# A graph kernel's cosine pass: GpSimd prunes 512 of 3327 columns of each block, ScalarE sums them, and VectorE makes a row's threshold behind its pruning

## The chip, the cores and the metric

The kernel runs on one core of a Trainium2 chip. The metric is the device time of one launch in microseconds (us). Where several runs are given, it is their median.

## What is computed

Four graph layers work on 3327 nodes with 64 features each and a full adjacency matrix. The change lies in the fourth, which runs the function below twice (`it` is 0, then 1). Here `H` is the adjacency (3327 x 3327, float32):

```python
cos = xn @ xn.T                                     # xn: normalised rows of x_comp
edge_scores = softmax(cos * H / TAU, axis=1)
edge_mask = (edge_scores >= th_edge) & comp_mask[:, None]
H_pruned = H * edge_mask
connectivity = H_pruned.sum(axis=1)                 # sum of each row
node_scores = softmax(connectivity * feat_mag / TAU)
...
vdeg = maximum(H_pruned.sum(axis=1), EPS)
edeg = maximum(H_pruned.sum(axis=0), EPS)           # sum of each column
transformed = x_final @ W
agg = H_pruned.T * dv_isqrt[None, :] @ transformed  # the "down" pass
msg = dv_isqrt[:, None] * (H_pruned @ agg)          # the "up" pass
```

## The kernel before

The nodes are padded to 26 blocks of 128 rows (`NB` = 26). A block of the adjacency is 128 x 3328 float32, 1664 KB, and lies in a slot of SBUF while it is used. The adjacency doesn't fit, so that each pass (edge, att, cos, down, up, in this order, twice) streams it again from HBM. SyncE issues all loads from one queue, in the order of the passes; each waits until the slot's last user is done. The cosine pass has four slots (`slot0` to `slot3`), and its last four blocks stay in them for the down pass.

The cosine pass goes over the blocks k = 0 to 25. For each:

- TensorE makes the cosines in four pieces of 2 x 416 columns, in three buffers of PSUM. `piece_place` says which buffer, and how many pieces ago it was last used. In its queue the column sums of block k-2 (`columns`, which multiplies the pruned slot by ones) stand between the pieces: ahead of them are block k+1's first two pieces. When they are done, the slot is free for the load of block k+2 (`block_done`).
- VectorE multiplies each piece by the slot's columns into `prod[k % 2]` and takes its maximum (`product_piece`, L1311, shown as a CUSTOM instruction and an accumulator read). `product_max` (L1322) makes the row's maximum.
- ScalarE takes the exponentials in place with their row sum (L1063, `exps`).
- VectorE makes the threshold of a row in `cut` (L1449, `cut_of`): the row sum times `th_edge`, or something huge where the node is masked out.
- VectorE prunes the slot (L1457, `prune`): each element times (product >= threshold), and the row sum into `conn`. ScalarE takes the signs of product minus threshold into `arena` for the later passes (L1081), and says with `product_free` that the product buffer is free.

The work of two blocks overlaps: VectorE prunes block k-1 while ScalarE does block k's exponentials. The order on each engine is the order of the code, `cosine_pass` on VectorE. A first piece also waits for the pruning two blocks before, which reads the same product buffer.

Behind the pass, `conn` gives the node scores through a softmax, whose maximum and sum over the partitions GpSimd takes (L531, L533); before the change this is nearly all that GpSimd does. The down pass needs the features made from it. In these passes all engines' semaphore waits are written out by hand.

## Time and profile before

| | |
|---|---|
| time, median of 3 runs | 1784.53 us (1782.18 to 1786.14) |
| time of the profiled execution | 1784.21 us |
| its span, first to last instruction | 1782.4 us |
| TensorE busy | 1544.1 us (87%) |
| VectorE busy | 1195.5 us (67%) |
| ScalarE busy | 682.5 us (38%) |
| GpSimd busy | 4.0 us |
| the two cosine passes in the span | about 693 to 904 us and 1346 to 1555 us |
| mean granted TensorE clock | 0.95 of full speed |

An engine's share is over the whole span; the passes differ in what limits them, so the windows of a pass say more about it. The windows of the section below go from block 2's maximum to block 25's. In the profile, PE is TensorE, DVE is VectorE, ACT is ScalarE, POOL is GpSimd, SP is SyncE. What stands in brackets at the end of a timeline's row is the idle time of the engine before it and what ended it.

### The profile page before, as it was taken

The page shows a single profiled execution, that of the slowest core. Times are in us where ns is not written, and L with a number is a line of the kernel's source. Part 1 is how long each engine was busy: PE and PEld are TensorE (multiplying, and loading weights), DVE is VectorE, ACT ScalarE, POOL GpSimd, SP SyncE. Part 2 cuts the span into 40 slices and gives each one's busy share as a digit, 9 for nine tenths or more (in the row PEclk, how much of TensorE's full clock was granted, in tenths as well). Part 3 has the DMA queues.
Part 4 walks back from the last instruction along what each step waited for, and adds up shares of the span by engine and source line. Part 5 has one row for each costly group of instructions (what it writes and reads, how often), then busy time and mean ns, then how long its engine had stood idle before and what let it go on. Part 6 is the DMA issues. An engine that isn't in the chain of part 4 may idle for free.

```text
span 1782.4 us, 22339 instructions
## 1 busy us (share of the span) xinstructions
PE 1544.1 (87%) x9517; PEld 614.4 (34%) x9517; DVE 1195.5 (67%) x1684; ACT 682.5 (38%) x520; POOL 4.0 (0%) x17
## 2 busy tenths in 40 slices
PE   6789998999999998777787799999997777787895
PEld 2234433334443333222232344443333222232442
DVE  0000306777423997999988798027988999989897
ACT  0000101333113775777720242115666787700441
POOL 0000000000000000000000000000000000000000
PEclk9999999999999999878889999999999888799998
DMA  9979596799798993556569999999992566589994
GB/s 404 426 283 427 232 427 231 243 346 411 304 427 358 382 377 147 208 214 229 193 268 426 423 420 426 425 427 398 383 373 93 202 220 228 187 362 425 426 426 169
DMA packets 60611, 578.29 MB, mean 324 GB/s; under 512 B 6240, under 2 KB 6496, under 8 KB 20832
## 3 DMA queue, kind: packets, MB, share of 16 engines
q1 hardware_dynamic: 60512, 576.87, 80.9%
q8 instruction: 75, 1.23, 0.3%
q14 instruction: 24, 0.20, 0.0%
HBM read 575.14 MB, written 1.70 MB: 324 GB/s over the span
## 4 chain that ended last, share of the span: by engine, by line
PE 50%; DVE 28%; DMA 18%; ACT 2%; issue 2%; SPq 0%; DVEq 0%; POOL 0%; ACTq 0%
PE ps L548 47%; DVE pairs L1311 11%; DVE slot L1457 9%; DMA slot<-adj 9%; DMA arena<-adj_t 7%; DMA slot<-adj_t 2%; PE ps L891 2%; DVE slot L1485 1%; DVE slot L1499 1%; ACT pairs L1063 1%; DVE hats L1499 0%; DVE negmax L1322 0%; PE ps L590 0%; ACT arena L1081 0%; ACT hats L1100 0%
## 5 line engine op out<-in xcount | busy, mean ns | idle before, releaser
L1311 DVE CUSTOM_DVE_ANT_1 pairs<-ps,slot 128x832 f32<-128x832 f32 x352 | 345.5, 1021 | 29.8 <-PE ps L548 15.7
L548 PE MATMUL ps<-slot,cur 128*64 128x512 f32 (+1 forms) x1536 | 281.4, 515 | 31.6 <-DVE slot L1485 20.2
L548 PE MATMUL ps<-hats 64*128 64x416 f32 x832 | 224.7, 649 | 95.1 <-DVE max L1311 93.8
L1063 ACT ACTIVATE pairs<-pairs,negmax 128x3327 f32<-128x3327 f32 x88 | 270.3, 3071 | 71.5 <-DVE negmax L1322 71.3
L548 PE MATMUL ps<-arena 64*128 64x416 f32 (+1 forms) x1072 | 207.5, 524 | 0.4 <-DVE max L1311 0.4
L1081 ACT ACTIVATE arena<-pairs,cut 128x3328 fp8e4<-128x3328 f32 x52 | 159.9, 3074 | 87.2 <-DVE cut L1449 87.2
L1457 DVE SCALAR_TENSOR_TENSOR slot<-pairs,cut,slot 128x3327 f32<-128x3327 f32 x52 | 191.2, 3677 | 0.1
L548 PEld LDWEIGHTS ps<-slot,cur 128*64 128x64 f32 x1536 | 103.4, 137 | 205.6 <-issue 164.1
L548 PEld LDWEIGHTS ps<-hats 64*128 64x128 f32 x832 | 77.8, 215 | 233.0 <-DVE max L1311 184.7
L1131 DVE COPY pairs<-ps 128x512 f32<-128x512 f32 x3 | 2.1, 692 | 195.1 <-PE ps L548 195.1
L1100 ACT ACTIVATE hats<-ps 128x2048 int16<-128x2048 int16 (+1 forms) x28 | 42.1, 1556 | 231.3 <-PE ps L891 231.3
L548 PEld LDWEIGHTS ps<-arena 64*128 64x128 f32 (+1 forms) x1072 | 87.1, 175 | 121.3 <-DVE max L1311 62.4
L1485 DVE SCALAR_TENSOR_TENSOR slot<-arena,slot 128x3328 f32<-128x3328 int8 x28 | 101.5, 3626 | 19.2 <-DMA slot<-adj 19.2
L548 PE MATMUL ps<-slot,ones 128*32 128x416 f32 x832 | 106.3, 641 | 6.7 <-DVE slot L1457 6.7
L548 PE MATMUL ps<-pairs,hats 128*128 128x512 bf16 (+1 forms) x408 | 89.2, 341 | 7.1 <-DVE pairs L1264 4.3
L548 PE MATMUL ps<-pairs,arena 128*64 128x512 bf16 (+2 forms) x736 | 94.7, 372 | 0.1
L548 PE MATMUL ps<-slot,arena 128*64 128x512 f32 x480 | 88.4, 521 | 1.6 <-DMA slot<-adj 1.6
L1009 ACT ACTIVATE pairs<-ps 128x512 int16<-128x512 f32 x104 | 53.1, 517 | 92.5 <-PE ps L548 92.4
L1264 DVE TENSOR_SCALAR pairs<-ps 128x512 int16<-128x512 f32 x104 | 60.5, 590 | 36.3 <-PE ps L548 32.4
L942 ACT ACTIVATE pairs<-ps 128x640 f32<-128x640 f32 (+1 forms) x6 | 3.9, 652 | 198.4 <-PE ps L548 198.4
L1499 DVE SCALAR_TENSOR_TENSOR slot<-hats,slot 128x3328 f32<-128x3328 int8 x20 | 72.1, 3622 | 8.8 <-ACT hats L1100 5.8
L548 PE MATMUL ps<-arena,cur 128*64 128x512 f32 (+1 forms) x384 | 68.6, 513 | 1.1 <-DMA arena<-adj_t 1.0
(186 smaller groups left out, 1454.8 us busy)
## 6 DMA issues: line engine op xcount, KB each, us to landing
slot<-adj SPq DMA_DIRECT2D x162, 1664.0 KB, 8.9
slot<-adj_t SPq DMA_DIRECT2D x64, 1664.0 KB, 15.5
arena<-adj_t SPq DMA_DIRECT2D x26, 1664.0 KB, 23.5
arena<-adj_t SPq DMA_DIRECT2D x52, 832.0 KB, 6.5
arena<-adj SPq DMA_DIRECT2D x15, 1664.0 KB, 14.5
pairs<-adj SPq DMA_DIRECT2D x15, 1664.0 KB, 15.7
pairs<-adj_t SPq DMA_DIRECT2D x12, 1664.0 KB, 14.6
hats<-adj SPq DMA_DIRECT2D x8, 1664.0 KB, 15.0
```

The costliest lines, as they stand in the source:

```text
L548: return pe.matmul(o, l, r, start=start, stop=stop, skip_group_check=True)
L891: last = pe.transpose(ps[:, 4 * BANK + q * D:4 * BANK + (q + 1) * D].bitcast(BF16), sign_pairs[:, q * HALF + pair * P:q * HALF + (pair + 1 ...
L942: act.activation(agg_f[:, CHUNK_COLS[c]], ps[:, CHUNK_COLS[c]], ACT.Copy).then_inc(early_cols[c], 1)
L1009: act.activation(dst, bank(c, w), ACT.Relu).then_inc(relu_act, 1)
L1063: act.activation(bufs[b][:, 0:N], bufs[b][:, 0:N], ACT.Exp, bias=negmax[:, b:b + 1], accum_out=rowsum[:, b:b + 1]).then_inc(exp_done, 1)
L1081: act.activation(interleaved(sign_marks[:, row * NP:(row + 1) * NP]), halves(prod[k % 2][:, 0:NP]), ACT.Sign, bias=cut[:, k % 2:k % 2 + 1] ...
L1100: act.activation(turned[pair % 2][:, cols], ps[:, 4 * BANK:4 * BANK + HALF].bitcast(I16)[:, cols], ACT.Copy)\
L1264: dve.tensor_scalar(dst, bank(2 + c, w), 0.0, None, ALU.max).then_inc(relu_dve, 1)
L1311: dve.tensor_tensor_reduce(out=pieces3(bufs[k % len(bufs)], c), in0=pieces_psum(piece_place(name, k, c)[0]), in1=pieces3(slot_of(name, k), ...
L1457: dve.scalar_tensor_tensor(out=slot[:, 0:N], in0=prod[k % 2][:, 0:N], scalar=cut[:, k % 2:k % 2 + 1], in1=slot[:, 0:N], op0=ALU.is_ge, op1 ...
L1485: dve.scalar_tensor_tensor(out=slot, in0=interleaved(signs[:, row * NP:(row + 1) * NP]), scalar=0.0, in1=slot, op0=ALU.is_le, op1=ALU.mult ...
L1499: dve.scalar_tensor_tensor(out=slot, in0=interleaved(turned[k // 2 % 2].bitcast(I8))[:, k % 2], scalar=0.0, in1=slot, op0=ALU.is_le, op1=A ...
```

## The change

VectorE's pruning stops 512 columns before the end. GpSimd prunes these 512 in two instructions: marks (product >= threshold) into a tile of its own, then the slot's columns times the marks. ScalarE sums the 512 by row, one block late, behind the signs; the sums go into `conn_share`, which VectorE adds to `conn` behind the pass. In VectorE's queue a block's threshold moves from behind the next block's first piece to ahead of it, right behind the pruning. The waits that this needs are added: TensorE's column sums wait for GpSimd too, SyncE's loads for ScalarE's sum, and a piece for the marks two blocks before, which read its product buffer.

```diff
+SHARE = 512
...
@@ SyncE, late_stream
                     sp.wait_ge(block_done, EARLY_RING + free)
+                    behind = free - 1 - BASE[f"cos{it}"]
+                    if kind in ("cos", "down") and 0 <= behind < NB:
+                        sp.wait_ge(share_summed, it * NB + behind + 1)
...
@@ GpSimd
+            def prune_share(it, k):
+                slot = slot_of(f"cos{it}", k)
+                cols = slice(N - SHARE, N)
+                pool.wait_ge(row_cut, it * NB + k + 1)
+                if it * NB + k:
+                    pool.wait_ge(share_pruned, it * NB + k)
+                pool.tensor_scalar(share_marks[:, :], prod[k % 2][:, cols], cut[:, k % 2:k % 2 + 1], None, ALU.is_ge)\
+                    .then_inc(share_marked, 1)
+                pool.wait_ge(share_marked, it * NB + k + 1)
+                pool.tensor_tensor(slot[:, cols], slot[:, cols], share_marks[:, :], ALU.mult).then_inc(share_pruned, 1)
...
             for it in range(2):
                 node_softmax(2 * it)
+                for k in range(NB):
+                    prune_share(it, k)
                 node_softmax(2 * it + 1)
...
@@ TensorE, columns
                         pe.wait_ge(pruned, it * PRUNES + k + 1)
+                        pe.wait_ge(share_pruned, it * NB + k + 1)
...
@@ ScalarE
+                def sum_share(k):
+                    at = place(ROW_ORDER["cos"][k])
+                    act.wait_ge(share_pruned, it * NB + k + 1)
+                    if it * NB + k:
+                        act.wait_ge(share_summed, it * NB + k)
+                    act.activation(share_sink[:, :], slot_of(f"cos{it}", k)[:, N - SHARE:N], ACT.Copy,
+                                   accum_out=small["conn_share"][:, at:at + 1]).then_inc(share_summed, 1)
                 for k in range(NB):
                     exp_and_sign(k)
+                    if k:
+                        sum_share(k - 1)
+                sum_share(NB - 1)
...
@@ VectorE, product_piece
                             dve.wait_ge(pruned, g // 2 * PRUNES + k - 1)
+                            dve.wait_ge(share_marked, g // 2 * NB + k - 1)
...
@@ VectorE
             def cosine_pass(name, cut_of, prune):
                 for k in range(NB):
-                    product_piece(name, k, 0)
-                    if k > 1:
-                        cut_of(k - 1)
-                    for c in range(1, 4):
+                    for c in range(4):
                         product_piece(name, k, c)
                     if k == 1:
                         cut_of(0)
                     product_max(name, k)
                     if k:
                         prune(k - 1)
-                cut_of(NB - 1)
+                        cut_of(k)
                 prune(NB - 1)
...
-                    dve.scalar_tensor_tensor(out=slot[:, 0:N], in0=prod[k % 2][:, 0:N],
-                                             scalar=cut[:, k % 2:k % 2 + 1], in1=slot[:, 0:N], op0=ALU.is_ge,
+                    cols = slice(0, N - SHARE)
+                    dve.scalar_tensor_tensor(out=slot[:, cols], in0=prod[k % 2][:, cols],
+                                             scalar=cut[:, k % 2:k % 2 + 1], in1=slot[:, cols], op0=ALU.is_ge,
                                              op1=ALU.mult, accum_out=S["conn"][:, at:at + 1]).then_inc(pruned, 1)
...
                 dve.wait_ge(pruned, it * PRUNES + NB)
+                dve.wait_ge(share_summed, it * NB + NB)
+                link(dve.tensor_tensor(S["conn"], S["conn"], S["conn_share"], ALU.add))
```

On VectorE, from block 2's maximum to block 3's, the queue held this before (L1322 is the maximum, L1457 the pruning, L1311 a piece and its accumulator read, L1449 the threshold):

```order
L1322 TENSOR_REDUCE negmax<-max4 128x1 [waits piece_read]
L1457 SCALAR_TENSOR_TENSOR slot3,conn<-pairs,cut,slot3 128x3327 [waits row_cut]
L1311 ISA pairs,max4<-ps,slot1 128x2x416 [waits pruned,piece_ready,product_free,slot_loaded1]
L1311 ISA max4 128x1
L1449 SCALAR_TENSOR_TENSOR cut<-rowsum,blocked 128x1 [waits exp_done]
L1311 ISA pairs,max4<-ps,slot1 128x2x416 [waits piece_ready]
```

And it holds this now, at the same place (L1360, L1493, L1349 and L1484 are the same four):

```order
L1360 TENSOR_REDUCE negmax<-max4 128x1 [waits piece_read]
L1493 SCALAR_TENSOR_TENSOR slot3,conn<-pairs,cut,slot3 128x2815 [waits row_cut]
L1484 SCALAR_TENSOR_TENSOR cut<-rowsum,blocked 128x1 [waits exp_done]
L1349 ISA pairs,max4<-ps,slot1 128x2x416 [waits share_marked,pruned,piece_ready,product_free,slot_loaded1]
L1349 ISA max4 128x1
L1349 ISA pairs,max4<-ps,slot1 128x2x416 [waits piece_ready]
```

The threshold, with its wait for the exponentials, moved ahead of the next block's first piece, and that piece waits for one semaphore more.

On ScalarE, at the end of a pass, the queue held this before (L1063 exponentials, L1081 signs, L1070 the softmax's exponentials):

```order
L1063 ACTIVATE pairs,rowsum<-pairs,negmax 128x3327 [waits negmax_ready]
L1081 ACTIVATE arena<-pairs,cut 128x2x1664 [waits row_cut]
L1063 ACTIVATE pairs,rowsum<-pairs,negmax 128x3327 [waits negmax_ready]
L1081 ACTIVATE arena<-pairs,cut 128x2x1664 [waits row_cut]
L1070 ACTIVATE node_e,psum_<-node_z,ngmax 128x26 [waits soft_bias]
```

It holds this now (L1089, L1107, L1096 are these three, L1116 the new row sums):

```order
L1089 ACTIVATE pairs,rowsum<-pairs,negmax 128x3327 [waits negmax_ready]
L1107 ACTIVATE arena<-pairs,cut 128x2x1664 [waits row_cut]
L1116 ACTIVATE share_sink,conn_share<-slot1 128x512 [waits share_summed,share_pruned]
L1089 ACTIVATE pairs,rowsum<-pairs,negmax 128x3327 [waits negmax_ready]
L1107 ACTIVATE arena<-pairs,cut 128x2x1664 [waits row_cut]
L1116 ACTIVATE share_sink,conn_share<-slot2 128x512 [waits share_summed,share_pruned]
L1116 ACTIVATE share_sink,conn_share<-slot3 128x512 [waits share_summed,share_pruned]
L1096 ACTIVATE node_e,psum_<-node_z,ngmax 128x26 [waits soft_bias]
```

One row sum follows each block's signs, and two follow the last.

On GpSimd, at the same place, there are now the last blocks' marks (L546) and products (L549) ahead of the softmax's two reductions (L554, L556). Before, its queue held the reductions alone:

```order
L546 TENSOR_SCALAR share_marks<-pairs,cut 128x512 [waits share_pruned,row_cut]
L549 TENSOR_TENSOR slot2<-slot2,share_marks 128x512 [waits share_marked]
L546 TENSOR_SCALAR share_marks<-pairs,cut 128x512 [waits share_pruned,row_cut]
L549 TENSOR_TENSOR slot3<-slot3,share_marks 128x512 [waits share_marked]
L554 ISA
L554 ISA gmax<-pmax 128x1 [waits part_max]
L556 ISA gsum<-psum_ 128x1 [waits part_sum]
```

The row "L554 ISA" without operands tells GpSimd to change the set of functions that it runs; another stands ahead of the first marks of each pass. Before the change there is one in the whole program, at its start.

## Rows read from the trace of the kernel before

**Rows 1.** The page: each engine's busy time; the chain that ended last, by line.
```profile
PE 1544.1 (87%) x9517; PEld 614.4 (34%) x9517; DVE 1195.5 (67%) x1684; ACT 682.5 (38%) x520; POOL 4.0 (0%) x17
...
PE ps L548 47%; DVE pairs L1311 11%; DVE slot L1457 9%; DMA slot<-adj 9%; DMA arena<-adj_t 7%; DMA slot<-adj_t 2%; PE ps L891 2%; DVE slot L1485 1%; DVE slot L1499 1%; ACT pairs L1063 1%; DVE hats L1499 0%; DVE negmax L1322 0%; PE ps L590 0%; ACT arena L1081 0%; ACT hats L1100 0%
```

**Rows 2.** Windows: length, busy PE PEld DVE ACT POOL, granted clock, DMA share, GB/s.
```profile
710.50:896.30 185.80, 141.78 (x740) 45.12 (x742) 177.17 (x277) 142.50 (x70) 0.00 (x0) 0.83 0.56 202
1363.50:1547.10 183.60, 144.10 (x744) 45.39 (x746) 177.02 (x278) 142.39 (x70) 0.00 (x0) 0.83 0.57 205
```

**Rows 3.** Timeline, VectorE, one block: start, length in us, instruction.
```profile
742.38 0.16 DVE L1322 TENSOR_REDUCE negmax<-max 128x1 f32<-128x4 f32 x1
...
746.38 1.02 DVE L1311 CUSTOM_DVE_ANT_1 pairs<-ps,slot 128x832 f32<-128x832 f32 x1 [0.24 <-DMA slot<-adj]
...
747.32 0.15 DVE L1449 SCALAR_TENSOR_TENSOR cut<-rowsum,blocked 128x1 f32<-128x1 f32 x1
747.40 1.02 DVE L1311 CUSTOM_DVE_ANT_1 pairs<-ps,slot 128x832 f32<-128x832 f32 x1
...
750.35 0.16 DVE L1322 TENSOR_REDUCE negmax<-max 128x1 f32<-128x4 f32 x1
```

**Rows 4.** Timeline, ScalarE, the same block.
```profile
742.57 3.07 ACT L1063 ACTIVATE pairs<-pairs,negmax 128x3327 f32<-128x3327 f32 x1
745.55 0.19 ACT L1063 ACTIVATION_READ_ACCUMULATOR pairs<-pairs,negmax 128x1 f32 x1
747.51 3.07 ACT L1081 ACTIVATE arena<-pairs,cut 128x3328 fp8e4<-128x3328 f32 x1 [1.78 <-DVE cut L1449]
```

**Rows 5.** Groups by line and form: count, busy us, mean ns, idle before.
```profile
L1457 DVE SCALAR_TENSOR_TENSOR slot<-pairs,cut,slot 128x3327 f32<-128x3327 f32 x52 | 191.2, 3677 | 0.1
L1449 DVE SCALAR_TENSOR_TENSOR cut<-rowsum,blocked 128x1 f32<-128x1 f32 x52 | 8.0, 155 | 2.4 <-ACT pairs L1063 2.4
L1063 ACT ACTIVATION_READ_ACCUMULATOR pairs<-pairs,negmax 128x1 f32 x88 | 16.5, 188 | 0.0
L958 ACT ACTIVATE arena<-arena 128x512 f32<-128x512 f32 x8 | 5.0, 629 | 16.2 <-DVE arena L1141 16.2
L1063 ACT ACT_TABLE_LOAD x2 | 2.6, 1283 | 0.0
```

**Rows 6.** Timeline, start of the first pass.
```profile
707.27 0.19 ACT L1063 ACTIVATION_READ_ACCUMULATOR pairs<-pairs,negmax 128x1 f32 x1
...
707.50 0.16 DVE L1449 SCALAR_TENSOR_TENSOR cut<-rowsum,blocked 128x1 f32<-128x1 f32 x1 [1.20 <-ACT pairs L1063]
```

**Rows 7.** Groups of GpSimd.
```profile
L531 POOL PARTITION_ALL_REDUCE gmax<-pmax x4 | 1.4, 351 | 1549.4 <-DVE pmax L1368 1549.4
L523 POOL MEMSET ones_b<- 128x512 bf16 x1 | 0.5, 530 | 0.0
```

**Rows 8.** Timeline, end of the first pass.
```profile
896.26 0.16 DVE L1322 TENSOR_REDUCE negmax<-max 128x1 f32<-128x4 f32 x1
...
903.85 0.19 DVE L1465 TENSOR_TENSOR imp<-conn,norm 128x26 f32<-128x26 f32 x1
```

**Rows 9.** Timeline, TensorE: column sums (slot,ones), pieces (hats); a window, columns as above.
```profile
736.56 2.86 PE L548 MATMUL ps<-slot,ones 128*32 128x416 f32 x16
...
742.36 1.60 PE L548 MATMUL ps<-slot,ones 128*32 128x416 f32 x16
...
747.46 0.97 PE L548 MATMUL ps<-hats 64*128 64x416 f32 x4 [2.60 <-DVE max L1311]
...
734.00:736.00 2.00, 2.00 (x8) 0.63 (x4) 1.97 (x4) 2.00 (x2) 0.00 (x0) 0.50 0.02 7
```

**Rows 10.** Issues of loads (timeline), and one in the chain (us to landing).
```profile
739.49 0.33 SPq L483 DMA_DIRECT2D slot<-adj  x1
...
852.01 8.40 DMA slot<-adj
...
1535.37 0.33 SPq L483 DMA_DIRECT2D slot<-adj  x1
```

More of the change, by code:

```diff
@@ L242, in build_program @@
                  ("mean", "var", "structural", "colsum", "imp", "comp", "blocked", "norm", "rnorm",
-                  "conn", "node_z", "node_e", "dv", "edeg")}
+                  "conn", "conn_share", "node_z", "node_e", "dv", "edeg")}
         tiny = {n: sb(n, 1, F32) for n in ("pmax", "gmax", "ngmax", "psum_", "gsum", "thr", "query_shift")}
         max4 = sb("max4", 2 * 4, F32)
+        share_marks = sb("share_marks", SHARE, BF16)
+        share_sink = sb("share_sink", SHARE, BF16)
         row_rz = sb("row_rz", 3, F32)
@@ L376, in build_program @@
         pruned = sem("pruned")
+        share_marked = sem("share_marked")
+        share_pruned = sem("share_pruned")
+        share_summed = sem("share_summed")
         product_free = sem("product_free")
@@ L480, in late_stream @@
                         sp.wait_ge(pruned, it * PRUNES + NB)
+                        sp.wait_ge(share_pruned, it * NB + NB)
                         sp.wait_ge(product_free, (2 * it + 2) * NB + 2)
```

## The prediction

> **What bounds the kernel now.** I read the page first: TensorE is busy 87% of the span and VectorE 67%, and the chain that ended last goes to VectorE's pieces and to its pruning (L1457) with 11% and 9% [rows 1]. Such shares are averages over stages, so I then asked for the windows of the two cosine passes from their third block on. There VectorE works 177.17 of 185.80 us and 177.02 of 183.60 us, ScalarE 142 us and TensorE 142 to 144 us at a mean granted clock of 0.83, and the DMA engines are a little over half busy [rows 2]. So in this stage VectorE sets the pace. The timeline of one block shows how [rows 3, 4]. Count from the start of the block's maximum M (742.38): the pruning of the block before starts at once, the next first piece at M+4.00 (746.38), then comes the threshold (747.32, which moves the second piece back by 0.08), and the next maximum is at M+7.97 (750.35). Of 24 such periods in a pass nearly all are 7.96 to 7.98 long. ScalarE's exponentials start at M+0.19 and their sum is read at M+3.36 (745.55 plus 0.19); the reader should see that the threshold, and the signs behind it, wait for nothing but their place in VectorE's queue: the signs start at 747.51, after 1.78 us in which ScalarE idled [rows 4].
>
> **VectorE's block after the change.** The pruning takes 3677 ns for 3327 columns and an instruction of that kind on one column 155 ns [rows 5], so 1.059 ns a column: 512 columns fewer save 0.54 us. By the queue alone the next first piece then starts at M+3.46. The threshold now stands ahead of it and needs the exponentials' sum: M+3.36, plus 0.04 until VectorE has it (at the pass's start the sum is read at 707.46, the threshold starts at 707.50 [rows 6]), plus 0.07 to 0.08 until the piece behind it starts (747.32 to 747.40): M+3.47. The two ends meet, so this wait costs 0.01. From the first piece to the maximum it takes 3.97, without the threshold in it 3.89. The period is 3.47 + 3.89 = 7.36, say 7.37. Of the 23 periods from block 2's maximum to block 25's, which took 185.7 us and 183.6 us [rows 2], 169.5 us each would be left: 16.2 + 14.1 = 30.3 us saved, if nothing else is late.
>
> **ScalarE.** Signs start at M+3.58 (0.18 behind the threshold), and what is behind them 2.97 later (745.55 less 742.57 is the pitch of an instruction of this length): M+6.55. A 512-column pass from tile to tile takes 629 ns, the reading of a sum 188 ns [rows 5], together about 0.73 of pitch: it ends at M+7.28. The next exponentials want to start at M+7.56. It is hidden with 0.28 to spare; every tenth above that would cost 0.1 x 46.
>
> **GpSimd.** Nothing in this trace has GpSimd read a wide tile. The nearest rows are a memset of 512 columns, 530 ns, and a reduction of one column over partitions, 351 ns [rows 7]. From below, two instructions at 0.53 take 1.1; with the second at twice that for its two inputs, 1.6; with semaphores 1.8. From above there is no row: the pair is hidden while it is shorter than the next block's pieces (3.9 us), because until then only TensorE's column sums (which wait for the later VectorE pruning anyway), ScalarE's sum and a piece two blocks on wait for it. I take 1.8 because the memset is the nearest row, and cost it at nothing. SyncE's new waits are in order behind ones that end later: ScalarE's sum ends at M+7.3 of the following block, the column sums behind that.
>
> **The pass's ends.** At the start, exponentials of block 1 are held up by the signs of block 0, and the threshold waits 1.20 us until 707.50 [rows 6], but one piece has run ahead of it. Now this piece is behind the threshold: 0.94 more, in each pass. At the end, today the last maximum is at 896.26 and the first step of the softmax at 903.85: M+7.59 [rows 8]. Now the last threshold is at M+3.40, the signs end their pitch at M+6.55, and two row sums of 0.73 and 0.78 follow, one behind the other: M+8.06; then the new addition, 0.04 + 0.23: M+8.33. That is 0.8 more, in each pass, and all that follows (softmax, features, the down stage with its loads) waits for it. Both ends and both passes: 2 x (0.94 + 0.8) = 3.5 us lost.
>
> **What is late next: the loads.** A slot is loaded again when TensorE has summed its columns. In every other block that sum stands behind two pieces that wait for VectorE. When the granted clock is 0.50 (1.2 GHz) the sum takes 2.86 us instead of 1.60, and ends 5.0 us behind the maximum at 734.41 (742.38 less a period): the load goes out at 739.49 [rows 9, 10], and block 7's first piece at 746.38 had its landing as releaser [rows 3]: 6.8 us later, M+11.9. Before the change that was just in time (two periods less 3.97 is 11.97). After it, it is wanted at 7.37 + 3.47 = M+10.85. Of the 20 such loads (ten a pass, 739.49 first, 1535.37 last [rows 10]) I took landing less maximum: most lie at 10.6 to 11.9, two at 12.7 and 13.6 (852.01, 8.40 to landing, which stalls the kernel now). Beyond 10.87 they add up to 7.9 us in the first pass and 3.8 in the second: 11.7 us of the gain go if TensorE's slow stretches stay as they are. If none is left, such a load goes out at M+2.6 and nothing is lost. The clock falls after TensorE has idled 2.60 us, run one piece of 0.97 and idled again (747.46 [rows 9]), and VectorE's shorter pruning takes about 0.5 of those 4.6 us away: same shape, a little less idle. So I stay near the upper end and take 9.
>
> Sum: -30.3 + 3.5 + 9.0 = -17.8 us. The profiled execution took 1784.2 us, 0.3 under the median of the three, so 1766.4 by its own time and 1767 against the median.
>
> **Rivals.** First, the clock no longer falls in most blocks: the 9 go and 1757.7 is left. For it speaks that TensorE's idle stretches shorten, against it that each late load makes a new one. Chance 0.15.
>
> Second, the ends of the pass cost more, because GpSimd is not ready. GpSimd has to change its set of functions before the first product of a pass and again ahead of the softmax's maximum. The first change has over 10 us of cover, the second only from the last product (M+5.4) to the maximum (M+9.1), 3.7 us. The nearest row is ScalarE's loading of a table, 1283 ns [rows 5]: hidden if it begins with the change, 2.6 us in both passes if it begins with the call. In the last block, too, VectorE's pruning starts together with GpSimd's marks; if one of them has to wait for the other, 0.5 to 1.1 us are added and the row sum slips as much: 2 us for both passes. Together 1768 to 1771. But the table is another engine's; a GpSimd load five times as long, 6.4 us from each of two calls on, adds 12.8: 1780. Chance 0.2. The Trainium skill, "GPSIMD Engine Reference", section Instruction dispatch, puts the first call of a freshly loaded function at about 6 us more; beginning with the change that would be 2.2 us a pass, beginning with the call 6 us a pass; no row here shows it. The Trainium skill, "SBUF — State Buffer", section Who interferes with whom, says that a VectorE instruction with two SBUF inputs and a GpSimd instruction that reads SBUF exclude each other for their whole length. The pieces have one input in PSUM, so by that rule GpSimd's work is free where I have put it, and costs where a pruning runs beside it: at the last block, and everywhere if the pair is longer than 3.9 us.
>
> Third, no change: TensorE's slow stretches grow until every second load binds and two blocks take 15.9 us as now. Only the ends remain, +3.5 us, 1788, at the edge of what can be told. Chance 0.07: the rows of loads speak against it, as their path alone allows 15.8 and mostly less.
>
> Fourth, slower: GpSimd is far from the memset's pace. Its products then run into VectorE's next pruning, or set the pace themselves. The point is 7.97 us for the pair with its semaphores, 3.9 for one instruction, seven times the memset. At 9 us a pair, 46 periods of 9 instead of 7.97 are 47 us, 1835. Chance 0.08; another 0.03 for smaller losses of the same kind, between 3.9 us and the point. The forecast keeps 0.47.
>
> **Numbers.** 0.2% (3.6 us) is about what can be told from no change here. Faster: forecast, first and second rival, 0.82. Same: 0.07. Slower: 0.11. The range goes from the first rival to the end of the second, 1756 to 1780, and leaves out the third and fourth. For the forecast alone it would be 1760 to 1772.
>
> **What would show it.** VectorE's period from maximum to maximum 7.37 where no load is late; the pruning 3.13; the threshold's idle before it below 0.1; first pieces of every second block with the load as releaser, 0.3 to 1 us. ScalarE: row sums 0.63 long and no maximum that waits for it. GpSimd's pair near 1.8 us and done before the next maximum. From the last maximum to the softmax's first step 8.3. Wrong would be the forecast if GpSimd's instructions are several times as long, if VectorE's pieces stretch beside them, or if the clock changes.

## The result, and the profile after

The changed kernel took 1796.18 us (median of four, 1793.98 to 1801.87), the kernel before on the same chip 1784.79 us: ratio 1.0071, 95% interval [1.0051, 1.0091]. It is slower by 11 us, where the prediction had 1767 us, 18 less. The profiled execution took 1801.87 us, the longest of the changed kernel's four, so that the sums below, made between the two profiles, come to +17.7 us instead of +11.4. The other three have no trace, so that it isn't shown in which stages the 6.3 us between the two sums lie. One execution of e3 below took 3291.44 us, at a granted clock of 1.0 and for a reason that the record doesn't show, and its ratio leaves it out.

The page answers to [rows 1]: GpSimd now works 153.8 us, and ScalarE's exponentials (L1089) have gone from 1% of the chain to 5%, while VectorE's pruning (L1493) has left it.

```profile
PE 1539.0 (86%) x9489; PEld 616.0 (34%) x9517; DVE 1173.0 (65%) x1686; ACT 715.9 (40%) x624; POOL 153.8 (9%) x121
...
PE ps L573 50%; DMA slot<-adj 12%; DVE pairs L1349 8%; DMA arena<-adj_t 7%; ACT pairs L1089 5%; DMA slot<-adj_t 2%; PE ps L917 2%; DVE slot L1522 1%; DVE slot L1536 1%; DVE pairs L1301 1%; POOL share_marks L546 1%; PE ps L842 0%; PE ps L615 0%; DVE hats L1536 0%; ACT arena L1107 0%
```

The windows from block 2's maximum to block 25's, which answer to [rows 2]: 185.80 us became 179.29 and 183.60 became 178.98. That is 11.1 us gained, a little over half of the 21.3 that the prediction had left here (30.3 less 9.0 for the loads). The granted clock is nearly as it was (0.83 and 0.85, before 0.83 twice), and GpSimd's 61 us lie beside the others.

```profile
712.39:891.68 179.29, 141.12 (x746) 44.86 (x746) 167.19 (x277) 157.41 (x115) 60.96 (x46) 0.83 0.58 210
1374.07:1553.05 178.98, 139.88 (x750) 44.78 (x746) 167.13 (x276) 157.41 (x115) 61.00 (x46) 0.85 0.58 210
```

**One block.** On VectorE's timeline (answers to [rows 3]) the maximum comes every 7.53 us where no load is late, not every 7.37. The threshold starts at M+3.39 (761.51), after 0.16 us in which VectorE waited for ScalarE, and the piece at M+3.63, 0.24 behind the threshold.

```profile
758.12 0.16 DVE L1360 TENSOR_REDUCE negmax<-max 128x1 f32<-128x4 f32 x1
758.20 3.14 DVE L1493 SCALAR_TENSOR_TENSOR slot<-pairs,cut,slot 128x2815 f32<-128x2815 f32 x1
...
761.51 0.16 DVE L1484 SCALAR_TENSOR_TENSOR cut<-rowsum,blocked 128x1 f32<-128x1 f32 x1 [0.16 <-ACT pairs L1089]
761.75 1.02 DVE L1349 CUSTOM_DVE_ANT_1 pairs<-ps,slot 128x832 f32<-128x832 f32 x1
...
765.65 0.16 DVE L1360 TENSOR_REDUCE negmax<-max 128x1 f32<-128x4 f32 x1
```

The chain through the same block says who sets this pace: it goes maximum, exponentials with the reading of their sum (L1089, x2), threshold, then a semaphore instruction of VectorE's queue (DVEq) and the piece. The pruning is not on it.

```profile
758.12 0.17 DVE negmax L1360
...
758.31 3.17 ACT pairs L1089 x2
...
761.51 0.06 DVE cut L1484
761.57 0.05 issue
761.62 0.05 DVEq L1348
761.67 0.08 issue
761.75 1.02 DVE pairs L1349
```

VectorE's waits in the first of the two windows: the 0.16 us comes in each of the 23 blocks, and what is lost to late loads (and to TensorE's pieces behind them) is 4.9 + 1.2 us. In the second window it is 3.7 again, and 4.4 + 1.4 us.

```profile
DVE pairs L1349 <- DMA slot<-adj: 4.9, 4, 1.6
DVE cut L1484 <- ACT pairs L1089: 3.7, 23, 0.2
DVE pairs L1349 <- PE ps L573: 1.2, 4, 0.4
```

The groups (as in [rows 5]): pruning 3143 ns as forecast; marks and product (L549) 1562 (median of 52) and 1090 ns, together 2.65 us against the 1.8 taken, but still hidden. The pair took half as much again as estimated, and in the blocks that cost nothing. The mean of 1789 ns for the marks is raised by four of about 4.5 us, the first and the last block's of each pass (702.11, 895.33, 1363.80 and 1556.70).

```profile
L1493 DVE SCALAR_TENSOR_TENSOR slot<-pairs,cut,slot 128x2815 f32<-128x2815 f32 x52 | 163.4, 3143 | 0.1
L546 POOL TENSOR_SCALAR share_marks<-pairs,cut 128x512 bf16<-128x512 f32 x52 | 93.0, 1789 | 267.9 <-DVE cut L1484 267.9
```

**The end of the pass** holds most of the loss. Before the change, the reduction over the partitions and the matmuls behind the softmax stood like this, the last maximum being at 896.26:

```profile
904.57 0.35 POOL L531 PARTITION_ALL_REDUCE gmax<-pmax  x1 [215.38 <-DVE pmax L1368]
907.90 1.53 PE L816 MATMUL ps<-cst,pairs 128*128 128x128 f32 x12 [1.00 <-ACT pairs L1090]
```

The timeline of all engines in the changed kernel, first pass, answers to them and to [rows 8]:

```profile
891.68 0.16 DVE L1360 TENSOR_REDUCE negmax<-max 128x1 f32<-128x4 f32 x1
...
895.26 3.15 DVE L1493 SCALAR_TENSOR_TENSOR slot<-pairs,cut,slot 128x2815 f32<-128x2815 f32 x1
895.33 4.51 POOL L546 TENSOR_SCALAR share_marks<-pairs,cut 128x512 bf16<-128x512 f32 x1 [6.25 <-DVE cut L1484]
...
899.92 1.09 POOL L549 TENSOR_TENSOR slot<-slot,share_marks 128x512 f32<-128x512 f32 x1
...
902.09 0.19 DVE L1502 TENSOR_TENSOR imp<-conn,norm 128x26 f32<-128x26 f32 x1
...
902.54 0.18 DVE L1403 TENSOR_REDUCE pmax<-node_z 128x1 f32<-128x26 f32 x1
...
910.96 0.38 POOL L554 PARTITION_ALL_REDUCE gmax<-pmax  x1 [9.94 <-issue]
...
914.31 2.82 PE L842 MATMUL ps<-cst,pairs 128*128 128x128 f32 x12 [7.45 <-ACT pairs L1127]
```

Three things stand here. The last marks began 0.07 us behind a pruning and took 4.51 us. The reduction over the partitions had its input at 902.73 and began at 910.96, 8.2 us later, with nothing but "issue" as the cause (time in which the engine waited for nothing that the profile shows). And the matmuls of the next stage, behind 7.45 us of idle, took 2.82 us at a granted clock of 0.50 (914.31 to 917.13); before, twelve of them took 1.53 at 1.00 (907.90 to 909.40). In the second pass the input is there at 1564.10 and the reduction starts at 1570.99, 6.9 us later:

```profile
1570.99 0.38 POOL L554 PARTITION_ALL_REDUCE gmax<-pmax  x1 [8.60 <-issue]
```

From the last maximum to the reduction it was 8.31 and 8.30 us before, now it is 19.28 and 17.94. That is 20.6 us more, of which 15.1 are the reduction's wait behind its input and 5.5 are the later input.

The 9.94 and 8.60 us are the change of functions, as e1 to e3 below show: the list of L554's instructions has two waits of this kind, one a pass, and the instruction that orders a change, the last at 1562.6; the first pass's stands at 901.24 in the trace.

```profile
L554 POOLq MODIFY_POOL_CONFIG  x6: 11/11/11, 1.6 to 1562.6; - x6
...
  issue: 18.5, 2
```

From the order to the first call that is 9.7 and 8.4 us.

### The profile page after: what moved, and what is told of

Same layout as the page of the kernel before. It is cut to its first block, busy times and chain, and to the rows that moved or that the text cites. A ratio compares the mean times of both kernels' runs of the same rounds, so it can differ in the third digit from the quotient of the medians.

```text
span 1799.8 us, 22731 instructions
## 1 busy us (share of the span) xinstructions
PE 1539.0 (86%) x9489; PEld 616.0 (34%) x9517; DVE 1173.0 (65%) x1686; ACT 715.9 (40%) x624; POOL 153.8 (9%) x121
## 4 chain that ended last, share of the span: by engine, by line
PE 53%; DMA 21%; DVE 16%; ACT 6%; issue 2%; POOL 1%; SPq 0%; DVEq 0%; ACTq 0%
PE ps L573 50%; DMA slot<-adj 12%; DVE pairs L1349 8%; DMA arena<-adj_t 7%; ACT pairs L1089 5%; DMA slot<-adj_t 2%; PE ps L917 2%; DVE slot L1522 1%; DVE slot L1536 1%; DVE pairs L1301 1%; POOL share_marks L546 1%; PE ps L842 0%; PE ps L615 0%; DVE hats L1536 0%; ACT arena L1107 0%
## 5 line engine op out<-in xcount | busy, mean ns | idle before, releaser
L1349 DVE CUSTOM_DVE_ANT_1 pairs<-ps,slot 128x832 f32<-128x832 f32 x352 | 342.8, 1020 | 30.9 <-PE ps L573 18.3
L1089 ACT ACTIVATE pairs<-pairs,negmax 128x3327 f32<-128x3327 f32 x88 | 270.0, 3069 | 105.5 <-DVE negmax L1360 105.5
L573 PE MATMUL ps<-hats 64*128 64x416 f32 x832 | 220.2, 642 | 91.6 <-DVE max L1349 90.4
L1107 ACT ACTIVATE arena<-pairs,cut 128x3328 fp8e4<-128x3328 f32 x52 | 159.8, 3072 | 12.7 <-DVE cut L1484 12.7
L1493 DVE SCALAR_TENSOR_TENSOR slot<-pairs,cut,slot 128x2815 f32<-128x2815 f32 x52 | 163.4, 3143 | 0.1
L1522 DVE SCALAR_TENSOR_TENSOR slot<-arena,slot 128x3328 f32<-128x3328 int8 x28 | 101.5, 3625 | 23.8 <-DMA slot<-adj 23.8
L546 POOL TENSOR_SCALAR share_marks<-pairs,cut 128x512 bf16<-128x512 f32 x52 | 93.0, 1789 | 267.9 <-DVE cut L1484 267.9
L554 POOL PARTITION_ALL_REDUCE gmax<-pmax x4 | 1.5, 364 | 1143.0 <-DVE pmax L1403 1124.5
```

What stands on the lines that cost most here:

```text
L546: pool.tensor_scalar(share_marks[:, :], prod[k % 2][:, cols], cut[:, k % 2:k % 2 + 1], None, ALU.is_ge)\
L573: return pe.matmul(o, l, r, start=start, stop=stop, skip_group_check=True)
L1089: act.activation(bufs[b][:, 0:N], bufs[b][:, 0:N], ACT.Exp, bias=negmax[:, b:b + 1], accum_out=rowsum[:, b:b + 1]).then_inc(exp_done, 1)
L1107: act.activation(interleaved(sign_marks[:, row * NP:(row + 1) * NP]), halves(prod[k % 2][:, 0:NP]), ACT.Sign, bias=cut[:, k % 2:k % 2 + 1] ...
L1349: dve.tensor_tensor_reduce(out=pieces3(bufs[k % len(bufs)], c), in0=pieces_psum(piece_place(name, k, c)[0]), in1=pieces3(slot_of(name, k), ...
L1493: dve.scalar_tensor_tensor(out=slot[:, cols], in0=prod[k % 2][:, cols], scalar=cut[:, k % 2:k % 2 + 1], in1=slot[:, cols], op0=ALU.is_ge, ...
```

## The experiments

Each ratio is to runs of the kernel before on the same chip: 1784.53 us for e1 to e4, 1785.20 for e6, e7, e9 and e10, 1784.45 for e5, e8 and e11, 1785.37 for e12. In the diffs the counts of the semaphore waits, which follow from the number of shared blocks, are left out, and the constants for the first and the last shared block are written as numbers.

**e1: no share in the last two blocks.** VectorE prunes blocks 24 and 25 whole; GpSimd is finished, and its functions are changed back, about two blocks earlier.

```diff
-                for k in range(NB):
+                for k in range(24):
                     prune_share(it, k)
...
-                    cols = slice(0, N - SHARE)
+                    cols = slice(0, N - SHARE if k < 24 else N)
```

> The change, but blocks 24 and 25 of each pass are pruned whole by VectorE as before, so that GpSimd's last product of a pass is that of block 23. Theory (switch): what costs is GpSimd's change of its set of functions behind its last product: 9.7 us until the softmax's maximum can start, 8.2 of them exposed, and about 2.5 more in which TensorE works at a granted clock of 0.50 after that wait. Here the change begins some 13 us earlier and is hidden; the marks of the last block, stretched from 1.56 to 4.5 us beside VectorE's pruning, fall away too (3 us). Expected 2 x (8.2 + 2.5 + 3) less 2 x 1.1 for the whole prunings: 26 us under the changed kernel, about 1770, faster than before. Rival (port alone): only the stretched marks matter: 6 us less, 1790. Rival (body): the loss is in the pass itself: no gain, 1796.

1772.35 us (1768.62 to 1778.36), ratio 0.9927 [0.9912, 0.9942]. Two blocks a pass, four of 52, turn 0.7% slower into 0.7% faster: 23.8 us. GpSimd's rows at this pass's end say where: the reduction now waits for its input and for nothing else.

```profile
900.54 0.38 POOL L566 PARTITION_ALL_REDUCE gmax<-pmax  x1 [19.07 <-DVE pmax L1417]
```

From the last maximum (891.96) to it are 8.58 us, in the second pass 8.57. The change of functions is ordered at 1531.0 in the second pass, 17 us ahead of the reduction, and can't be seen. The bodies (the windows from block 2's maximum to block 25's) are as in the changed kernel: 179.53 and 179.22 us.

**e2: the kernel before, and one GpSimd instruction behind the last threshold.** It works on a single column, which nobody reads; its own semaphore is left out below.

```diff
             for it in range(2):
                 node_softmax(2 * it)
+                pool.wait_ge(row_cut, it * NB + 26)
+                pool.tensor_scalar(tick[:, :], eps_t[:, :], 2.0, None, ALU.mult)
                 node_softmax(2 * it + 1)
```

> The kernel before, with one GpSimd instruction more in each pass: a one-column tensor_scalar that waits for the last threshold. It computes nothing that is used. It makes GpSimd change its set of functions twice a pass, the second time ahead of the softmax's maximum, at about 4.1 us behind the last row maximum. Switch theory: the maximum over partitions then starts 9.7 us later, at 13.8 instead of 8.3, and the clock's fall adds about 2: 7 to 8 us a pass, 1800. Rival (the delay came from long instructions before it, not from the change): within 1 us of before, 1785.

1804.88 us, ratio 1.011 [1.0096, 1.0125]: 20 us for two instructions on one column each, against the 14 to 16 expected. From the last maximum to the reduction are 16.70 and 17.50 us. GpSimd's timeline:

```profile
899.67 3.72 POOL L542 TENSOR_SCALAR tick<-eps_t 128x1 f32<-128x1 f32 x1 [210.74 <-DVE cut L1455]
912.44 0.38 POOL L533 PARTITION_ALL_REDUCE gmax<-pmax  x1 [9.06 <-issue]
```

The change alone, with no pruning moved, costs nearly all that the end lost: 17.6 us up to the reduction, where the changed kernel lost 20.6. The row also shows the other price: this instruction ran beside a pruning (899.60 to 903.28) and ended 0.11 us behind it.

**e3: the same instruction behind the threshold of block 15.** The edit is e2's with 16 in place of 26.

> As e2_switch_late, but the extra instruction waits for the threshold of block 15, some 80 us ahead of the softmax. Switch theory: the same changes of the set of functions are made, but hidden: as before, 1785 within 2. Rival (a change costs wherever it stands, for instance because loading the functions disturbs other engines or loads): 5 us or more above before.

1784.79 us, ratio 0.9998 [0.999, 1.0007]. The instruction takes 0.27 us, the reduction comes 83.41 us behind it and starts with its input. A change of functions costs nothing when nobody calls for 83 us, and in e1 nothing could be seen of it with 17 us; how little is enough was not tried. It also says that the loading doesn't begin with the call, else it would be seen here too.

**e4: the changed kernel with the old order of the thresholds** (the first piece of block k+1 ahead of the threshold of block k).

```diff
-                    for c in range(4):
+                    product_piece(name, k, 0)
+                    if k > 1:
+                        cut_of(k - 1)
+                    for c in range(1, 4):
                         product_piece(name, k, c)
...
-                        cut_of(k)
+                cut_of(NB - 1)
```

> The changed kernel with the threshold back behind the next block's first piece, as before; the share of GpSimd and ScalarE stays. By VectorE's queue a period is 7.97 less 0.54 = 7.43 us, where the changed kernel has 7.53, and the piece at the pass's start runs ahead again (1 us a pass): 46 x 0.10 + 2 = 6 to 7 us less, 1790. Rival: ScalarE's signs and row sum slip behind with the threshold, its exponentials start 0.7 us late in each block and something waits for them: period 7.6 or more, 1798 or more.

1793.96 us (1788.52 to 1802.25), ratio 1.0056 [1.0035, 1.0077]: 2.2 us less than the changed kernel, where 6 to 7 were expected, and the intervals overlap. The period where no load is late is 7.42 us, the starts (from the first maximum to block 2's) take 13.29 instead of 14.47, but more blocks wait for loads: the bodies are 180.75 and 180.12 us, longer than with the new order. (This profile too, 1802.25 us, is the longest of its kernel's.) Beyond 46 periods of 7.42 us that is 19.5 us of late loads, where the changed kernel has 11.9 beyond 46 of 7.53. So the shorter period couldn't be cashed while the loads were late.

**e5: the kernel before with the new order alone** (the edit to `cosine_pass` of the change, nothing else).

> The kernel before with the new order alone: the threshold of block k is made behind the pruning of block k-1 instead of behind the first product piece of block k+1; VectorE still prunes all 3328 columns and GpSimd and ScalarE do nothing new. Theory of the waits: a product piece directly behind a threshold loses about 0.1 to 0.2 us a block, because its own waits are worked off behind the threshold (in the changed kernel the piece began 0.23 us behind the threshold, 7.53 us a block against 7.42 with the old order). Then a block takes 8.05 to 8.15 us instead of 7.97, the stretch from the first maximum to the third grows from 13.3 to about 14.4 us in each pass, some of the body's loss is taken back by the late loads, and the kernel takes 1790 to 1795 us. Rival: the 0.11 us belongs to the share's own waits (the one on share_marked ahead of the piece), not to the order; then a block takes 7.97 us and only the two starts are lost, 1787 us.

1787.62 us, ratio 1.0016 [1.0007, 1.0025]. Both forecasts of the period missed (the rival's time, 1787, came for another reason than it gave): it is 7.89 us in most blocks, so the order itself gives 0.07 to 0.08 back, as the prediction had it. VectorE's timeline:

```profile
759.38 0.16 DVE L1322 TENSOR_REDUCE negmax<-max 128x1 f32<-128x4 f32 x1
759.46 3.68 DVE L1454 SCALAR_TENSOR_TENSOR slot<-pairs,cut,slot 128x3327 f32<-128x3327 f32 x1
...
763.06 0.15 DVE L1446 SCALAR_TENSOR_TENSOR cut<-rowsum,blocked 128x1 f32<-128x1 f32 x1
763.38 1.02 DVE L1311 CUSTOM_DVE_ANT_1 pairs<-ps,slot 128x832 f32<-128x832 f32 x1 [0.17 <-issue]
```

Here the threshold stands directly behind the pruning, at M+3.68, and has no wait; the piece is at M+4.00, where it was before the change. With the threshold ahead of it or without, it starts 0.24 us behind the pruning's end (763.14; before 746.14 and 746.38), so the threshold runs in time that passes anyway. The kernel is slower all the same because of the starts (14.44 instead of 13.30 us, twice), which the bodies (184.70 and 182.55 us) just about return, and because of the 1.3 us that the two passes lose from the reduction to the down pass. Whether that belongs to the order is not shown: e10, whose ends are those of the kernel before, has 1.1 there.

**e6: e1, with the piece's waits on the marks, the product buffer and the load put ahead of the threshold.**

```diff
                     if k:
                         prune(k - 1)
+                        if k + 1 < NB:
+                            g = PRODUCTS.index(name)
+                            dve.wait_ge(product_free, g * NB + k + 2)
+                            dve.wait_ge(share_marked, ...)
+                            landed(dve, name, k + 1)
                         cut_of(k)
```

> e1_share24 with three of the waits of a first piece (product buffer, marks, landing) moved ahead of the threshold in VectorE's queue; they are then passed while VectorE prunes or the exponentials run. In the changed kernel the piece starts 0.23 us behind the threshold's start where I had taken 0.07. Theory: the sequencer works off the piece's waits one after the other, behind the threshold that has just been let go, at some 0.04 each: the period falls from 7.53 to about 7.41, 46 x 0.12 = 5 us less than e1_share24, at most, and less where loads bind: 1768 to 1772. Rival: the 0.23 is the wait for the draining of the pruning, which stays where it was: period 7.53, no gain.

1776.96 us (1772.07 to 1780.09), ratio 0.9955 [0.9943, 0.9967]; a miss, and the rival's period: 7.53 us. The threshold started at M+3.49 instead of M+3.39, and the piece where it had been. The median is 4.6 us above e1's at the same period; while loads come late the runs of one such kernel spread over 8 to 14 us. The profiles show how: e6's, the shortest of its six, has 5.6 us beyond 46 periods of 7.53, e1's, the longest of its six, 12.4. More than that I can't say of it.

**e11: e7 (below), with the piece's wait for the pruning ahead of the threshold.** The edit is one line, a wait on `pruned`, moved from `product_piece` to ahead of `cut_of(k)`.

> From e7, with the wait of the product piece on the pruning of the block before put ahead of the threshold instead of behind it. If the 0.23 us between threshold and piece is this wait being worked off, the piece comes nearer to the threshold and the threshold doesn't move: a period of about 7.44 us, 1760 us. Rival, by e6_waits_first, where a moved wait only delayed the threshold by what it saved behind it: 7.53 us, 1763 to 1764 us, and the 0.2 us is a price of having waits between two instructions, wherever they stand.

1768.05 us, ratio 0.9905 [0.9889, 0.992]; both numbers missed, it is slower than either. The chain of one block:

```profile
759.07 3.17 ACT pairs L1104 x2
...
762.27 0.02 DVEq L1498
762.29 0.04 issue
762.34 0.06 DVE cut L1501
...
762.57 1.02 DVE pairs L1365
```

With a second wait ahead of it, the threshold no longer waits for the exponentials itself: a semaphore instruction does, and the threshold follows 0.07 us behind that, at M+3.46. The piece kept its distance (0.23), and the period became 7.59 us. e6 and e11 together: in neither was a wait that was moved ahead of the instruction on the path hidden, although what it waited for had happened before (in e11 the pruning ended at 762.09, the exponentials at 762.25).

**e12: e7 with a share of 384 columns instead of 512.**

> e7 with GpSimd's share cut from 512 columns to 384, so that VectorE's pruning takes 0.14 us more. e5 (the order alone, 7.89 us a block) and the changed kernel (7.53) differ by 0.36 us, though the pruning is 0.54 us shorter; 0.16 to 0.18 us are missing. Theory: with the shorter pruning the threshold no longer stands behind VectorE's pruning but waits for ScalarE's row sum, until 3.39 us behind the maximum, and the first piece starts 0.23 us behind the threshold; the sum of ScalarE, not the pruning, sets the period. By e5's distances the pruning of 2944 columns would let the piece start 3.60 us behind the maximum, the threshold lets it start at 3.62: the period stays 7.52 to 7.54 us and the time that of e7, 1763 to 1765 us. Rival: VectorE's own queue sets the period, and the 0.16 us is the price of the additional wait on share_marked: then the period grows by the whole 0.14 us to 7.66, 46 x 0.14 = 6 us, 1769 to 1770 us.

1765.77 us (1764.87 to 1766.94), ratio 0.9893 [0.9876, 0.9909], against 1763.67 of e7. The theory's period came, 7.53 us in nearly all blocks of both passes, its time (1763 to 1765) not quite; the median is 2 us above e7's, where the rival wanted 6, and the ratios' intervals overlap. VectorE's timeline:

```profile
758.30 0.16 DVE L1377 TENSOR_REDUCE negmax<-max 128x1 f32<-128x4 f32 x1
758.38 3.27 DVE L1510 SCALAR_TENSOR_TENSOR slot<-pairs,cut,slot 128x2943 f32<-128x2943 f32 x1
...
761.69 0.16 DVE L1501 SCALAR_TENSOR_TENSOR cut<-rowsum,blocked 128x1 f32<-128x1 f32 x1
761.93 1.02 DVE L1366 CUSTOM_DVE_ANT_1 pairs<-ps,slot 128x832 f32<-128x832 f32 x1
...
765.84 0.16 DVE L1377 TENSOR_REDUCE negmax<-max 128x1 f32<-128x4 f32 x1
```

The pruning is 0.13 us longer, the threshold stays at M+3.39, the piece (761.93) at M+3.63. In this order ScalarE's sum sets the pace, and a quarter of GpSimd's work bought nothing.

**e7: e1, and six matmuls on zeros behind TensorE's pieces in every second block.** They add zero to a buffer of PSUM and fill part of the time in which TensorE idles.

```diff
                         if k + 1 < NB:
                             piece(k + 1, 2)
+                        if (k + 1) % 2 == 1:
+                            for _ in range(6):
+                                mm(bank(6), zeros_b[:, :], ones_b[:, :], start=False)
```

> e1_share24 with six TensorE products of zeros (512 columns, added to the column sums' banks, so that nothing changes) behind the third piece of every second block, in the gap in which TensorE idles. Theory (clock): TensorE's granted clock stays up in the passes, column sums take 1.6 instead of 2.9 us, loads go out 2 us earlier and no first piece waits for a landing: the 12.4 us of a body beyond 23 x 7.53 in two passes go, e1 less 10 or so: 1762. Rival (the loads are late by the DMA rate): the clock rises but the stalls stay: 1772. Second rival: the products of zeros delay pieces: slower than 1775.

1763.67 us (1761.78 to 1765.39), ratio 0.988 [0.9868, 0.9893]: 8 to 9 us less than e1. The windows from block 2's maximum to block 25's:

```profile
710.83:884.65 173.82, 143.04 (x822) 44.53 (x818) 166.82 (x276) 157.41 (x115) 58.34 (x44) 0.97 0.61 216
1351.31:1524.44 173.13, 142.26 (x822) 44.38 (x818) 166.72 (x277) 157.41 (x115) 58.33 (x44) 0.98 0.61 217
```

The granted clock is 0.97 and 0.98 instead of 0.83 and 0.85, and 23 x 7.53 = 173.2 us: the late loads are gone, and one wait of 0.6 us for a piece of TensorE's is all that VectorE still loses beside the threshold's. TensorE was never short of time; at 1.2 GHz its column sums gave the slots back too late. In the block whose maximum is at 734.97 in the changed kernel the sum took 2.74 us and the next load went out at M+4.96; in the same block of e7 (maximum at 734.11) it took 1.60 us and the load went out at M+2.59.

**e10: the same matmuls in the kernel before.**

> The kernel before with the same products of zeros. Clock theory: there, loads stall VectorE only 2.6 and 0.5 us beyond its period in the two passes, so at most 3 us are to be had: 1782 to 1785. If it gains more, the products of zeros help outside the cosine pass, and e7_fill has to be read against this.

1782.44 us, ratio 0.9987 [0.9978, 0.9995]. Before the change there was little to give back: the two bodies stood 3.2 us above 46 periods of 7.96, and now stand 0.8 above. The filler is worth 8 to 9 us only together with the shorter period.

**e9: e1, with the marks held back until the next block's maximum,** so that they run beside a pruning.

```diff
                 pool.wait_ge(row_cut, it * NB + k + 1)
+                pool.wait_ge(negmax_ready, (2 * it + 1) * NB + k + 2)
```

> e1_share24, but GpSimd's marks of block k also wait for the maximum of block k+1, so that they start together with VectorE's pruning of block k instead of ahead of it. Port theory: VectorE's pruning, which has two inputs in SBUF, keeps GpSimd's marks out for its whole length: marks of 4.5 to 4.7 us instead of 1.56 in all 48 cases. A first piece two blocks on waits for them: about M+4.8 instead of 3.6, so the period grows to 8.6 or more and the kernel to 1772 + 46 x 1.1 = 1820 or more. Rival (the stretched marks are only those next to a change of GpSimd's functions): marks 1.56, over at M+1.8, before the pruning is; period 7.53, 1772.

1822.42 us, ratio 1.0212 [1.0199, 1.0225]. GpSimd's groups by form:

```profile
L559 POOL TENSOR_SCALAR share_marks<-pairs,cut 128x512 bf16<-128x512 f32 x48 | 207.6, 4326 | 180.5 <-DVE negmax L1375 168.1 <-DVE cut L1499 12.4
```

The marks end about 1.4 us behind the pruning (763.72 to 766.86, marks 763.96 to 768.29), and alone they take 1.56 us: it looks as if they didn't run slower, but waited for its end. The pruning keeps its 3.14 us, as it started first. The period is 8.81 us.

**e8: e7 with the old order,** the parts that helped put together.

> The parts that helped, put together: share of GpSimd in blocks 0 to 23 only (the last two pruned whole by VectorE), six matmuls on zeros per second block that keep the granted clock up, and the old order of the thresholds. From e7 (1763.67 us), less 46 periods x 0.11 us, less 2 x 1.17 us at the starts: 1756 to 1757 us, with a period of 7.42 us and starts of 13.3 us. Rival: with the shorter period the late loads bind, as in e4 (whose bodies were not shorter by what its period promised); then the bodies stay at 173 us, only the starts come back, and it takes 1761 to 1763 us.

1758.02 us (1755.60 to 1759.52), ratio 0.9848 [0.9835, 0.9862]: 26 us faster than the kernel before, and the best of all, though 1 us over the expected 1756 to 1757. The first window, at full clock, is 23 periods of 7.42 us (the second took 171.01 us, at 0.98):

```profile
710.29:880.89 170.60, 137.83 (x808) 43.19 (x818) 164.69 (x277) 154.91 (x116) 58.33 (x44) 1.00 0.62 221
```

## Why the prediction was wrong

It chose the right stage, and what it costed on VectorE, ScalarE and GpSimd alone was nearly right: the pruning (3.14 us), the row sums (0.61 and 0.19 us, done before the next maximum in every block but the last), GpSimd hidden. The sign was lost at the end of the pass. Between the profiles, for both passes:

| term | predicted | measured |
|---|---|---|
| 46 periods | -30.3 | -22.9 |
| late loads | +9.0 | +11.9 |
| starts | +1.9 | +2.3 |
| ends, last maximum to the softmax's maximum | +1.6 | +20.6 |
| from there to the down pass | 0 | +4.3 |
| elsewhere | 0 | +1.5 |
| sum | -17.8 | +17.7 |

(46 x 7.53 = 346.4 against 369.3 before; 358.3 - 346.4 = 11.9. The prediction's 0.8 for an end is 8.33 less 7.59, which is 0.74; the sum's 3.5 would be 3.4.) From -17.8 to +17.7 are 35.5 us: 19.0 of them are the ends, 7.4 the period, 4.3 the way to the down pass.

**The step that failed** is the pass's end: "That is 0.8 more, in each pass, and all that follows ... waits for it." GpSimd's change of functions was costed at nothing there. It was the second rival, with 3.7 us of cover and prices from 1.3 to 6.4 us, and 1780 us as its far end. Shown: the change takes 8.4 to 9.7 us from its order to the first call (e2: 9.06 us of idle), and the cover was not 3.7 us but 1.5 (901.24 to 902.73), because the last product ended at M+9.33 (901.01) and not at M+5.4. Of the 20.6 us in the table 15.1 are this wait. e2 puts the change in alone and costs 20 us, e3 moves it away from the call and costs nothing, e1 takes it off the end together with the stretched marks, and gains 23.8. The Trainium skill, "GPSIMD Engine Reference", section Instruction dispatch, allows about 6 us for the first call of a freshly loaded function, counted from the order without the wait for an event; counted so, the two calls here take 8.2 and 6.9 us, and the measurement decides.

**The port** was named too, at 0.5 to 1.1 us a pass. By the trace the last marks took 4.51 us instead of 1.56, so 2.95 us, and the softmax's first step came at M+10.41 instead of the 8.33 predicted. e9 shows the same in every block. Where both read SBUF, the pruning with two inputs, they exclude each other for an instruction's whole length: this is what the Trainium skill, "SBUF — State Buffer", section Who interferes with whom, states, and the trace agrees: 4.33 us on average beside a pruning against 1.56 beside the pieces. The prediction had cited the rule and then priced it at 1.1 us at most; with the pruning 3.14 us long and started first, it should have been nearly 3.

**The period** was 7.53 where the step said "The two ends meet, so this wait costs 0.01." The row sum came when it said (M+3.36) and the threshold too (M+3.39), but the piece came 0.24 behind the threshold, not "0.07 to 0.08": that distance was read from a piece that has no waits of its own but TensorE's, and the first piece has four more. What exactly the 0.24 us consist of stays open; the chain shows a semaphore instruction in them. In e5 nothing is lost, as the piece is held until 0.24 behind the pruning's end anyway, and e12 shows that in the new order the pruning is off the path. So the new order ties each period to ScalarE's sum, and 0.16 us a block (7.4 us in all) is the price; the old order has 7.42, and the new one would have had 7.35 without it (e5's 7.89 less 0.54, an estimate). That the threshold can't be helped by moving waits is what e6 and e11 show.

**Late loads** were the right mechanism, and e7 shows that TensorE's clock is their cause. That the size is near, 11.9 us against 9.0, is partly luck: the 9.0 were for a period of 7.37 us, and e4, at 7.42, has 19.5 in its profile. They also differ from one execution to the next (5.6 us in e6's profile and 12.4 in e1's, at the same period), and the changed kernel's profile is its longest. The first rival, that the clock would no longer fall, needed e7's filler to come true. **Behind the softmax** the prediction had nothing. The long wait of the change let TensorE idle and start the next stage at half speed: 2.1 and 1.3 us, by the distance from the reduction to the down pass in the changed kernel less that in e1 (8.76 less 6.64, 8.49 less 7.19), or 3.4 of the 4.3 us. e1's own distance is 0.9 us above that of the kernel before, and like the 1.5 "elsewhere" this stays open; executions of one kernel differ by as much.

e8's time follows from the terms: without the end, the late loads and the order's 0.11 us a block, its two bodies are 27.7 us shorter than before, and 1784.2 less 27.7, plus 1.1 at the ends, is 1757.6 us; the median was 1758.02, the profiled execution itself 1755.60.

## What to carry to other kernels

Giving a helper engine elementwise work means asking not only whether the work hides, but what the helper must do next and whether it is ready for it: here 2.7 us of work a block was free and the way back to the other function kept a serial stretch waiting for 8.2 and 6.9 us, so the last pieces of a shared job belong to the engine that doesn't have to change. When an instruction is moved ahead of another in a queue, take the distance between them from a pair of which the second has the same waits, not from the nearest pair of the same names. And where a stage is near the pace of a resource that is slower when it idles, a shortening pays only as far as that resource follows: the same filler gained 2 to 3 us before the change and 8 to 9 behind it.

## What the runs showed of the hardware

- GpSimd going from elementwise instructions back to the reduction over partitions: 9.94, 8.60 and 9.06 us of idle, nothing if the call comes 83 us later (e3).
- A GpSimd instruction on one column took 3.72 us beside a pruning of 3.68 us (e2) and 0.27 us with no pruning beside it (e3).
- A comparison of 512 float32 columns on GpSimd took 1562 ns and a product of float32 by bfloat16, 512 columns, 1090: the one with a single input was the slower.
- In a queue where the waiting instruction is on the path, a second wait ahead of it cost 0.07 us though it was fulfilled already (e11, M+3.46 against M+3.39).
- With six short matmuls in every second block the granted clock went from 0.83 to 0.97 and more, at no cost that the traces show: VectorE's period is 7.53 us with them and without.
